# Product-key attention: the dense heads' pieces widened from 256 to 512 tokens, their mask made by ScalarE and TensorE, and the causal mask added by a matmul

## The reference, cut to what matters

```python
def _L3_ffn_ref(x, Wq_pk, pk_keys, Wq, keys_table, values_table, Wo):
    # HEADS = 8, NUM_KEYS = 64, so 4096 rows of a table per head
    q = (x @ Wq_pk).reshape(b, n, 2, HEADS, 32).transpose(2, 0, 1, 3, 4)
    sim = jnp.einsum('pbnhd,pkhd->pbnhk', q, pk_keys)
    scores, idx = jax.lax.top_k(sim, 16)
    score = scores[0][..., :, None] + scores[1][..., None, :]     # 256 pairs
    final_scores, pk_idx = jax.lax.top_k(score, 16)               # the best 16 pairs
    kv_scores = jax.nn.softmax(final_scores)
    k = jnp.einsum('bnhk,bnhkd->bnhd', kv_scores, keys_table[ind])
    v = jnp.einsum('bnhk,bnhkd->bnhd', kv_scores, values_table[ind])
    sim = jnp.einsum('bihd,bjhd->bhij', q, k)
    sim = jnp.where(causal, sim, neg)
    attn = jax.nn.softmax(sim, axis=-1)
    out = jnp.einsum('bhij,bjhd->bhid', attn, v)
    return out.reshape(b, n, HEADS * 64) @ Wo
```

## Time and profile before

| | |
|---|---|
| median of 3 runs | 15191.99 us (15181.57 to 15207.99) |
| the profiled execution | 15184.2 us |
| its span, first to last instruction | 15182.0 us |
| mean granted TensorE clock | 0.713 |
| busy over the span | DVE 68%, PE 66%, POOL 52%, ACT 39% |

### The profile page before, as it was taken

How to read it: one execution, slowest core, us unless ns; L and a number is a source line. 1 busy time by engine, 2 the same in 40 slices (tenths; PEclk the granted TensorE clock), 3 DMA queues, 4 the chain that set the end, 5 groups by cost and what they waited for, 6 DMA issues and landing times.

```text
span 15182.0 us, 143792 instructions
## 1 busy us (share of the span) xinstructions
PE 9984.7 (66%) x39356; PEld 5998.2 (40%) x39356; DVE 10276.2 (68%) x24001; ACT 5847.3 (39%) x13853; POOL 7907.9 (52%) x6892
## 2 busy tenths in 40 slices
PE   1564555555456643777777777777777777777777
PEld 1351222122131222445445445445445445444444
DVE  3334888888838657776676676676676676676662
ACT  0113333333310122454454454444444444444453
POOL 3000677676500003766666666666666666666662
PEclk9555777777757765677777777677677777677776
DMA  1000223222200001111111111111111111111110
GB/s 23 0 14 9 98 110 109 96 109 98 89 10 11 9 4 39 49 46 50 45 46 50 46 45 49 45 45 49 46 45 49 46 46 50 46 45 49 46 47 21
DMA packets 305126, 731.80 MB, mean 48 GB/s; under 512 B 130243, under 2 KB 170738, under 8 KB 269915
## 3 DMA queue, kind: packets, MB, share of 16 engines
q0 software_dynamic: 201216, 405.72, 10.3%
q1 hardware_dynamic: 103178, 317.81, 6.2%
HBM read 706.25 MB, written 8.42 MB: 47 GB/s over the span
## 4 chain that ended last, share of the span: by engine, by line
PE 34%; DVE 10%; ACT 10%; DVEq 4%; issue 3%; ACTq 0%
PE l3m_S L2286 8%; PE l3m_acc L2327 7%; PE l3m_O L2303 5%; PE l3m_DX L2316 4%; ACT l3m_spread L2416 4%; PE l3m_T L2293 4%; DVE l3m_W L2666 2%; ACT l3m_E L2455 2%; DVEq L2657 2%; PE l3m_DX L2314 1%; PE l3m_T L2252 1%; PE l3m_T L2273 1%; DVE l3m_side L2604 1%; ACT l3m_probT L2451 1%; DVEq L2574 1%
## 5 line engine op out<-in xcount | busy, mean ns | idle before, releaser
L2234 POOL DMA_INDIRECT l3m_got<-in_l_table,l3m_row x6144 | 5956.8, 970 | 3152.8 <-issue 1837.0
L2327 PE MATMUL l3m_acc<-l3m_W,l3m_values 128*128 128x256 f32 x4096 | 1869.3, 549 | 1678.2 <-DVE l3m_W L2666 1426.3
L2666 DVE SCALAR_TENSOR_TENSOR l3m_W<-l3m_DX,l3m_E 128x256 f32<-128x256 f32 x2048 | 863.2, 422 | 2133.5 <-ACT l3m_E L2455 2057.1
L2416 ACT ACTIVATE l3m_spread<-l3m_got,l3m_weight 128x128 f32<-128x128 f32 x6144 | 2082.6, 488 | 0.0
L2327 PEld LDWEIGHTS l3m_acc<-l3m_W,l3m_values 128*128 128x128 f32 x4096 | 837.2, 255 | 2022.6 <-DVE l3m_W L2666 1587.0
L2455 ACT ACTIVATE l3m_E<-l3m_DX 128x256 f32<-128x256 f32 x2048 | 787.0, 384 | 1946.9 <-PE l3m_DX L2316 1944.8
L2451 ACT ACTIVATE l3m_probT<-l3m_T 128x512 f32<-128x512 f32 (+3 forms) x1280 | 682.4, 533 | 1985.2 <-PE l3m_T L2293 1983.1
L1262 POOL TENSOR_TENSOR m_mul<-m_st,m_wide_c 128x2048 f32<-128x2048 f32 x256 | 1157.3, 4521 | 150.0 <-DVE m_st L1415 143.8
L2303 PE MATMUL l3m_O<-l3m_vo_g,l3m_probT 128*128 128x64 f32 x6528 | 978.6, 294 | 178.0 <-ACT l3m_probT L2451 178.0
L2303 PEld LDWEIGHTS l3m_O<-l3m_vo_g,l3m_probT 128*128 128x128 f32 x6528 | 895.5, 210 | 297.3 <-ACT l3m_probT L2451 251.5
L1295 PE MATMUL m_W<-m_mul,tower_ident 128*128 128x512 f32 (+1 forms) x1536 | 839.9, 669 | 207.3 <-POOL m_mul L1262 206.3
(11 more groups left out here) (673 smaller groups left out, 18827.3 us busy)
## 6 DMA issues: line engine op xcount, KB each, us to landing
m_wide_c<-l1a_c SPq DMA_DIRECT2D x256, 1024.0 KB, 4.7
l3m_got<-in_l_table,l3m_row POOLq DMA_INDIRECT x6144
l3m_values<-in_l_table SPq DMA_DIRECT2D x32, 512.0 KB, 4.5
l0i_img<-in_l_x SPq DMA_DIRECT2D x4, 1024.0 KB, 8.0
l2r_x<-l2a_hT SPq DMA_DIRECT2D x8, 512.0 KB, 5.4
qp_inw<-in_q_inw SPq DMA_DIRECT2D x1, 2336.0 KB, 8.0
l_kept<-l0t_xt,l0t_row POOLq DMA_INDIRECT x128, 2.2
l1a_c<-m_mul SPq DMA_DIRECT2D x16, 128.0 KB, 2.6
```

Source lines behind the costliest of these rows:

```text
L2234: pool.indirect_dma_start(got[:, unit % GOT, j, :], None, table, bass.IndirectOffsetOnAxis(ap=row[:, unit // QUAD % RING, unit % QUAD, j:j ...
L2327: pe.matmul(acc[:, 0:HALFQ], values[:, tile, :], W[:, k % 2, :], start=(tile == 0), stop=(tile == TILES - 1)).then_inc(blended, 1)
L2416: last = act.activation(spread[:, unit % 2, :, j], got[:, unit % GOT, j, :], ACT.Copy, scale=weight[:, g % RING, t, j:j + 1])
L2666: dve.scalar_tensor_tensor(W[:, k % 2, :], DX[:, 0:HALFQ], ABSENT, E[:, k % 2, :], ALU.is_gt, ALU.mult).then_inc(masked, 1)
```

## The change

Pieces are 512 tokens wide, so 1,024 instead of 2,048, two in a step, and DVE has no part in them. For a piece, `level` (PE) writes the sums of ranks over all 512 columns of `DX`; `lift` (ACT) makes `V = relu(100 - DX)` in bf16, which is 0 where the pair is among the 16 and positive elsewhere; `cross` (PE) then overwrites `DX` with the score (three matmuls) and adds `push @ V`, where `push` is -256 times the identity, so that absent pairs get at most -256; `grow` (ACT) takes the exponential of all 512 columns straight into `W`; and `blend` runs over 512 columns. `admit` and the buffers `E` go, `W` is one buffer, and `store` replaces `store_half` and runs once in a round. The causal mask becomes a bf16 matmul of the identity with the mask, accumulated onto `S` by `scores`; `peak` keeps only the maximum. The lists of PE and ACT are rewritten: ACT does `attend` first in a step, before `lift` and the first share of `part_up`.

```diff
-            mask, lanes = s.sb("mask", [P, P]), s.sb("lanes", [P, KEYS, TOPK], BF16)
+            mask, lanes = s.sb("mask", [P, 2, P], BF16), s.sb("lanes", [P, KEYS, TOPK], BF16)
...
+            push, least = s.sb("push", [P, P], BF16), s.sb("least", [P, 1])
...
+            dve.tensor_scalar(push[:], ident[:], -APART, None, ALU.mult)
+            dve.memset(least[:], ABSENT + 1.0)
...
-        return [64 * r + 4 * q + i for i in range(4)] if 0 <= r < ROWS else []
+        return [TILES * r + 2 * q + i for i in range(2)] if 0 <= r < ROWS else []
...
-        E, W, stage = u.sb("E", [P, 2, HALFQ]), u.sb("W", [P, 2, HALFQ]), u.sb("stage", [KV, CH])
+        V, W, stage = u.sb("V", [P, CH], BF16), u.sb("W", [P, CH]), u.sb("stage", [KV, CH])
...
-                    last = pe.matmul(S[:, c * CH:hi], qT[k:k + D, slot, t * P:(t + 1) * P],
-                                     kvT[kind][k:k + D, c * CH:hi], start=True, stop=True)
-                last.then_inc(scored, 1)
+                    pe.matmul(S[:, c * CH:hi], qT[k:k + D, slot, t * P:(t + 1) * P],
+                              kvT[kind][k:k + D, c * CH:hi], start=True, stop=(c < i // 4))
+                pe.matmul(S[:, i * P:(i + 1) * P], mask[:, 0, :], mask[:, 1, :], start=False,
+                          stop=True).then_inc(scored, 1)
...
+            def level(k):
+                if k % TILES == 0:
+                    pe.wait_ge(taild, k // TILES + 1)
+                if k:
+                    pe.wait_ge(grown, k)
+                pe.matmul(DX[:], sel[:, k % TILES, :], ranksT[:, k // TILES % 2, :],
+                          start=True, stop=True).then_inc(levelled, 1)
+
             def cross(k):
-                pe.matmul(DX[:, 0:HALFQ], sel[:, tile, :], ranksT[:, r % 2, lo:lo + HALFQ], start=True, stop=True)
+                pe.wait_ge(lifted, k + 1)
                 for i, x in enumerate((high, mid, tail)):
-                    last = pe.matmul(DX[:, HALFQ:], sel[:, tile, :], x[:, r % 2, lo:lo + HALFQ],
-                                     start=(i == 0), stop=(i == 2))
-                last.then_inc(crossed, 1)
+                    pe.matmul(DX[:], sel[:, k % TILES, :], x[:, k // TILES % 2, :], start=(i == 0), stop=False)
+                pe.matmul(DX[:], push[:], V[:], start=False, stop=True).then_inc(crossed, 1)
...
-                pe.wait_ge(masked, k + 1)
-                pe.matmul(acc[:, 0:HALFQ], values[:, tile, :], W[:, k % 2, :],
-                          start=(tile == 0), stop=(tile == TILES - 1)).then_inc(blended, 1)
+                pe.wait_ge(grown, k + 1)
+                pe.matmul(acc[:], values[:, tile, :], W[:], start=(tile == 0),
+                          stop=(tile == TILES - 1)).then_inc(blended, 1)
...
                 if todo:
-                    piece(todo.pop(0))
-                    piece(todo.pop(0))
+                    onward(todo[0])              # blend(k - 1), level(k)
...
+                    for c in range(max(3, depth[n] // 4 + 1)):
+                        if c <= depth[n] // 4:
+                            flip(n, c)
+                        if todo and c == 0:
+                            cross(todo[0])
+                        if todo and c == 1:
+                            onward(todo[1])
+                        if todo and c == 2:
+                            cross(todo[1])
+                        if c <= depth[n] // 4:
+                            mixing(n, c)
...
+            def lift(k):
+                act.wait_ge(levelled, k + 1)
+                act.activation(V[:], DX[:], ACT.Relu, bias=least[:], scale=-1.0).then_inc(lifted, 1)
+
             def grow(k):
                 act.wait_ge(crossed, k + 1)
-                act.activation(E[:, k % 2, :], DX[:, HALFQ:], ACT.Exp).then_inc(grown, 1)
+                act.activation(W[:], DX[:], ACT.Exp).then_inc(grown, 1)
...
-                if todo:
-                    grow(todo.pop(0))
-                part_up(unit, 0)
                 if n is not None:
                     attend(n)
                 if todo:
-                    grow(todo.pop(0))
-                part_up(unit, 1)
...
+                    lift(todo[0])
+                part_up(unit, 0)
+                for c in range(max(3, depth[n] // 4 + 1) if n is not None else 3):
+                    if n is not None and c <= depth[n] // 4:
                         take_flip(n, c)
...
+                    if todo and c == 0:
+                        grow(todo[0])
+                        part_up(unit, 1)
+                    if todo and c == 1:
+                        lift(todo[1])
+                        part_up(unit, 2)
+                    if todo and c == 2:
+                        grow(todo[1])
...
-                at = S[:, i * P:(i + 1) * P]
-                dve.tensor_tensor(at, at, mask[:], ALU.add)
-                dve.drain()
...
-            def admit(k):
-                dve.wait_ge(grown, k + 1)
-                if k >= 2:
-                    dve.wait_ge(blended, k - 1)
-                dve.scalar_tensor_tensor(W[:, k % 2, :], DX[:, 0:HALFQ], ABSENT, E[:, k % 2, :],
-                                         ALU.is_gt, ALU.mult).then_inc(masked, 1)
...
+            def store(g):
+
+                dve.wait_ge(blended, TILES * (g + 1))
+                if g:
+                    dve.wait_ge(placed, g)
+                dve.wait_ge(t_taken, T_at["inverse", g - 1] + 1)
+                dve.tensor_tensor(stage[:], acc[:], invT[:, g % 2, :], ALU.mult).then_inc(staged, 1)
```

More of the change, by code:

```diff
@@ L1998, in l3_ffn, with fold_keys @@
             wq, wo = s.sb("wq", [P, HEADS, 2 * D]), s.sb("wo", [P, HEADS, D])
-            mask, lanes = s.sb("mask", [P, P]), s.sb("lanes", [P, KEYS, TOPK], BF16)
+            mask, lanes = s.sb("mask", [P, 2, P], BF16), s.sb("lanes", [P, KEYS, TOPK], BF16)
             sel, counts = s.sb("sel", [P, TILES, P], BF16), s.sb("counts", [P, 2, TOPK], BF16)
-            fold_keys(nc, A, ident, wsim, iota, wq, wo, mask, lanes, sel, counts)
-            mix_heads(nc, A["l3_table"], h, hT, ident, ones, wsim, iota, wq, wo, mask, lanes, sel, counts)
-def fold_keys(nc, A, ident, wsim, iota, wq_all, wo_all, mask, lanes, sel, counts):
+            push, least = s.sb("push", [P, P], BF16), s.sb("least", [P, 1])
+            fold_keys(nc, A, ident, wsim, iota, wq, wo, mask, lanes, sel, counts, push, least)
+            mix_heads(nc, A["l3_table"], h, hT, ident, ones, wsim, iota, wq, wo, mask, lanes, sel, counts, push,
+                      least)
+def fold_keys(nc, A, ident, wsim, iota, wq_all, wo_all, mask, lanes, sel, counts, push, least):
     with Scope(nc, "l3w") as w:
@@ L2039, in _ @@
             pool.drain()
-            pool.memset(mask[:], 0.0)
+            pool.memset(mask[:, 1, :], 0.0)
             pool.drain()
-            pool.affine_select(out=mask[:], in_=mask[:], compare_op=ALU.is_ge, fill=-FAR, base=0,
+            pool.affine_select(out=mask[:, 1, :], in_=mask[:, 1, :], compare_op=ALU.is_ge, fill=-FAR, base=0,
                                pattern=[[-1, P]], channel_multiplier=1)
@@ L2084, in attended, with mix_heads @@
     return kind, g
-def mix_heads(nc, table, h, hT, ident, ones, wsim, iota, wq, wo, mask, lanes, sel, counts):
+def mix_heads(nc, table, h, hT, ident, ones, wsim, iota, wq, wo, mask, lanes, sel, counts, push, least):
     wsim_h = wsim[:].rearrange("d (p h k) -> d h p k", p=2, h=HEADS)
@@ L2325, in blend, with onward @@
                     pe.wait_ge(staged, k // TILES)
-                pe.wait_ge(masked, k + 1)
-                pe.matmul(acc[:, 0:HALFQ], values[:, tile, :], W[:, k % 2, :],
-                          start=(tile == 0), stop=(tile == TILES - 1)).then_inc(blended, 1)
-            def piece(k):
+                pe.wait_ge(grown, k + 1)
+                pe.matmul(acc[:], values[:, tile, :], W[:], start=(tile == 0),
+                          stop=(tile == TILES - 1)).then_inc(blended, 1)
+            def onward(k):
                 if k >= 1:
                     blend(k - 1)
-                cross(k)
+                level(k)
             def turn_dense(r):
@@ L2356, in _ @@
                 if todo:
-                    piece(todo.pop(0))
-                    piece(todo.pop(0))
+                    onward(todo[0])
                 elif r == ROWS and q == 0:
-                    blend(64 * ROWS - 1)
+                    blend(TILES * ROWS - 1)
                 made = made_at(r, q)
@@ L2366, in _ @@
                     pe.wait_ge(expd, n + 1)
-                    for c in range(depth[n] // 4 + 1):
-                        flip(n, c)
-                        if todo:
[L2370 to L2373, removed]
+                    for c in range(max(3, depth[n] // 4 + 1)):
[9 more added lines that the diff above has]
+                            mixing(n, c)
+                elif todo:
+                    cross(todo[0])
+                    onward(todo[1])
+                    cross(todo[1])
                 if made is not None:
@@ L2660, in scale @@
```

(8 more changed lines are left out.)

38 lines of the change are left out of this document (7 added, 31 removed).

## The result

The changed kernel takes 14,021.05 us (median of 4 runs, 14,018.11 to 14,023.34), against 15,190.17 for the kernel before in the same comparison. The ratio is 0.9228, with a 95% interval of 0.9214 to 0.9242. Predicted were 14,050 us and a range of 13,900 to 14,450.

A forecast was written before the change was run, and what follows sets the result against it. POOL's gathers were to bound the changed kernel: a floor of 13,956 us (15,184 less 1,228) plus 32 rounds of 3 us gave 14,052, say 14,050 us, range 13,900 to 14,450. The other engines' chain was put at 229 to 244 us a round.

The forecast's parts named there:

- POOL takes over as the bound: Stage with pieces: POOL's gathers set the pace, 243.6 to 251 us a round, 13,950 to 14,200 us; chance 0.66.
- the floor: Whole kernel: 15,184 us less the 1,228 us that POOL can give back of its waits for part_up, 13,956 us.
- The 3 us a round added for unevenness: On top of POOL's 243.6 us a round, since heavy rounds want 258: 246.5 taken, 32 x 3 us in all.
- The other engines' chain: PE, ACT and DVE without POOL's bound: 229 to 244 us a round, the lower half under POOL's 243.6.
- round 31: Kernel before, a round without top-k work on DVE for a next one: 238.4 us, the start of the sum giving 235.
- DVE's long steps: Steps with rank or decode, where a late peak can make attend wait: 0 to 15 us a round added.
- ACT's gain in work: lift and grow, 1.283 us a piece for 0.768: 16.5 us a round, 527 us in the stage, all counted in the path.
- The mask: Causal mask as a PE matmul in scores: 2.5 us a round added, 5 taken off for DVE's add.
- ScalarE's order: attend moves ahead of lift and share 0 of part_up; a late peak delays those two and the ring; no size given.
- Rival C: Slower: crossings find ACT in part_up and PE idle, 15,410 us, or table loads, some 16,700; chance 0.05 together.
- Rival B: The chain of PE and ACT paces the stage, 256 to 271 us a round: 14,500 us, far end 14,820; chance 0.27.
- The signs: POOL's part_up wait under 250 us, PE's longest regular wait under 3, clock 0.78 or more, DVE busy about 5,250 us.

The follow-up runs named there:

- the 12-gather run: Changed kernel with 12 of the 16 gathers of a unit, the last four rows taken from the first four: 13,431 us, 0.8842 of the kernel before.
- The halved version: Changed kernel with 12 of 16 gathers, and level, cross, lift and grow in two halves of 256 columns: 13,529 us, against 13,431 without the halves.
- the four parts: Changed kernel with rank's two 2,048-element DVE operations each done as four of 512 elements: 13,908 us, 0.9156 of the kernel before.

## Why the prediction was right

The error is 29 us. The mechanism, that POOL's gathers take over as the bound, is shown; that the number is so close is partly luck, since terms that were off cancel. They are worth taking one by one.

**POOL takes over as the bound: right.** 13,956 us was the floor worked out from gathers, gaps and the first filling of the ring. The stage ends up on it: POOL's busy time and gaps are 6,038.3 + 1,869 us, and it waits 27. But the floor moved. The gathers are 81 us and the gaps 32 us longer than before, the waits 18 us below the 45 that were allowed for, and the first gather starts 6 us later: 13,956 became 14,057. The gaps are longer because fewer of them lie hidden in a wait; why the gathers are longer is told in the last section. That the last stretch shortens was not in the sum: from the last gather to the end it is 238 us, where it was 274. 13,956 + 101 - 36 = 14,021 us, so POOL's own terms make up the whole time. The 3 us a round added for unevenness, 96 us in all, stood for something that didn't happen, and came out near the floor's net shift of 65 us by luck.

**The other engines' chain: right in the sum, wrong in its terms.** 229 to 244 us a round were predicted, and 228.4 is what the 12-gather run shows. But the prediction built this from round 31, for which it had 235 us, and that round takes 194.9 us there; and for DVE's long steps it added 0 to 15 us, where round 15 takes 32 more than round 31. The two errors cancel. The sum had no term for the clock: the granted clock of round 31 went from 0.78 to 0.95, and PE is busy 163 us in it where it was 193, with more columns to do. Since POOL sets the pace in the changed kernel, these errors cost the forecast nothing.

**ACT's gain in work: durations right, weight too high.** `lift` takes 0.683 and `grow` 0.594 us, where 0.686 and 0.597 were taken from other rows, and ACT's busy time in the stage grows by 451 us, where 527 were predicted. All of the 16.5 us a round was put in the path. The halved version adds 197 us to ACT's busy time and costs 97, so half would have been nearer, some 8 us; that is an estimate, since the halved version adds work to two crossings and not a new one. No table load occurs in the stage (the last of the program starts at 5,820 us), so what the Trainium skill states in "ScalarE: Activation LUTs", section "Table sets: the hidden batching unit", is borne out here: Relu and Exp alternate 1,024 times without one. The same page's rule that relu and multiply belong on VectorE is what the experiment with `lift` on DVE follows, and the measurement decides against it here: the two instructions last 0.690 and 0.683 us, and the choice is worth 646 us in the changed kernel and 1,238 where POOL isn't the bound.

**The mask: right.** 5 less 2.5 us a round was predicted; 3.5 was measured in the chain where POOL doesn't hide it, and 1.4 in the kernel before.

**What the prediction missed: ScalarE's order.** It named the place, that `attend` moves ahead, but gave it no price and said that a failure would most likely lie there. In the chain without POOL's bound it carries 1,537 us, more than the whole gain. That the gain comes from taking DVE out of the path, which the prediction argued from round 31, is only half the account: with DVE out and the old order of ACT the chain takes 14,968 us, 242 less than the old kernel with the same 12 gathers; with the new order and `lift` in DVE's list it takes 14,669, 541 less; with both changes 13,431, 1,779 less. Each needs the other. Nor is the order alone a gain, as the kernel before with `attend` first shows. Which part of PE's new order needs it (that `scores` comes before `cross`, or `level` apart from `cross`) was not tried.

**Rival C**, crossings that find ACT in `part_up`: the waits of `cross` and `blend` are 174 and 140 us over 2,048 crossings, 0.15 us each; it needed 1.3. **Rival B** had 14,500 us and a far end of 14,820: with `lift` on DVE the kernel takes 14,667 and is in it, and with `attend` late it is beyond it, at 14,968 even with 12 gathers. **The signs** that were named came, one of them in part: POOL's wait is 27 us, the clock in the stage 0.83, and DVE is busy 5,371 us; PE's longest regular wait is 2.0 us in the mean, but single ones last 7.6 us.

## What to carry to other kernels

When several engines work through lists in order, look for a round or an edge of the loop where one engine's side work is missing: it shows what that engine's place in the path costs before anything is changed. Look at what else differs there, though, the clock above all: here the round foretold the sum and not its terms. Where an operation stands in a list matters far more than what it costs there; when a list of one engine is rewritten, go through the others' lists against it, and price each exchange as everything that now stands ahead of the instruction that somebody waits for. Work out the busy time of the engine that will be next, since it caps the gain; and then measure the other changes with that cap lifted, or they all read as nothing.

## What the runs showed of the hardware

POOL's time for a gather depends on what DVE does when it starts. It is 0.944 us in the median. Two of `rank`'s operations of 2,048 bf16 elements, L2591 and L2595, hold it up. The timeline of the changed kernel:

```profile
9847.83 1.23 DVE L2591 TENSOR_TENSOR l3m_hot<-l3k_lanes,l3m_whereb 128x2048 bf16<-128x2048 bf16 x1
9848.29 1.58 POOL L2240 DMA_INDIRECT l3m_got<-in_l_table,l3m_row  x1 [0.30 <-issue]
...
9848.97 2.28 DVE L2658 TENSOR_REDUCE l3m_kv<-l3m_spread 128x128 f32<-128x2048 f32 x1
...
9850.17 0.94 POOL L2240 DMA_INDIRECT l3m_got<-in_l_table,l3m_row  x1 [0.31 <-issue]
9851.34 1.22 DVE L2595 TENSOR_TENSOR l3m_hot<-l3m_hot,l3k_counts 128x2048 bf16<-128x2048 bf16 x1
9851.42 1.95 POOL L2240 DMA_INDIRECT l3m_got<-in_l_table,l3m_row  x1 [0.30 <-issue]
```

The first gather above ends 0.81 us after L2591 does, and the last one 0.81 after L2595. Of the 256 gathers in this trace that start inside one of the two, 254 end 0.81 to 0.82 us after it. Together the 256 take 164 us more than as many median gathers; the expectation of the four parts had counted 146 gathers and 130 us. A gather that has run for 0.26 us or more when L2591 starts is not held; it takes 0.94 to 0.99 us. Nor is one that starts inside the sum of L2658, which has one input in SBUF and lasts 2.27 us: of 537 that start at least 0.3 us before its end and meet neither of the two, none takes over 1.0 us.

One hold can lead to the next. A gather held by L2591 puts the next but one 0.08 us behind the start of L2595, as above, when `sum_up` stands between the two. That happens 89 times in the changed kernel and never in the one before, and 117 gathers take over 1.6 us where 24 did. With it the gathers' time above the median is 238 us where it was 157, which is the 81 us by which the floor moved.

Parts of 512 elements, four of which take DVE about 1.44 us together instead of 1.23, give POOL 124 us back. The Trainium skill says in "GPSIMD Engine Reference", section "Key points", that GpSimd shares its SBUF interfaces with VectorE and contends with instructions that have two SBUF inputs or use the two-port mode. The trace agrees: both operations have two inputs in SBUF and L2658 has one. It adds that a gather's time on POOL grows by the hold, too. With POOL as the bound, 54 us more on DVE's list for 113 less in the kernel was a good exchange.
